# Attention with a message layer on one core: POOL makes three residuals before the attention and adds up a ninth tile in the first group of each chunk

## The reference

```
h    = relu(layernorm(x))
hs   = LN1(h);  ht = LN1(h_target)               # scale ln1_scale, bias ln1_bias
q    = (ht Wq + bq) / sqrt(32);  k = hs Wk + bk;  v = hs Wv + bv      # 8 heads of 32
p    = softmax over sources of (q k^T, -1e30 where there is no edge)
y    = LN2(ht + (p v) Wo + bo)
out  = x + y + gelu(y W1) W2                     # W1 256 x 1024, W2 1024 x 256
```

## Time and profile before

| | us |
|---|---|
| median of 3 runs | 499.89 |
| lowest, highest | 499.8, 501.54 |
| profiled execution | 502.69 |
| its span, first to last instruction | 500.8 |

### The profile page before, as it was taken

One profiled execution on the slowest core, in us unless ns is written; L12 is line 12 of the kernel. 1 busy time (PEld: TensorE's weight loads), 2 busy tenths in 40 slices (PEclk: granted clock), 3 DMA queues, 4 the chain that ended last, 5 costly groups with the idle time before them and its releaser, 6 DMA issues.

```text
span 500.8 us, 10602 instructions
## 1 busy us (share of the span) xinstructions
PE 477.0 (95%) x4364; PEld 245.4 (49%) x4364; DVE 416.5 (83%) x616; ACT 376.4 (75%) x455; POOL 309.9 (62%) x153
## 2 busy tenths in 40 slices
PE   3899979999999999999999999999999799999995
PEld 1466633333433343333433343333345688888884
DVE  5788579999999999999999999998997577565252
ACT  4786978998988998988998998999994370727150
POOL 2000008995998999999999998999999300000000
PEclk9899998999999999999999999999999899999998
DMA  8997689822633674222763300160000100202021
GB/s 254 250 192 115 125 247 403 297 43 44 211 58 55 68 172 80 43 45 48 82 171 66 64 3 3 36 178 2 1 1 3 45 21 23 84 2 84 0 85 45
DMA packets 53231, 46.94 MB, mean 94 GB/s; under 512 B 35454, under 2 KB 46108, under 8 KB 52668
## 3 DMA queue, kind: packets, MB, share of 16 engines
q1 hardware_dynamic: 50672, 37.30, 28.0%
q0 software_dynamic: 2480, 8.92, 10.7%
q10 hardware_dynamic: 28, 0.01, 0.0%
HBM read 31.93 MB, written 14.81 MB: 93 GB/s over the span
## 4 chain that ended last, share of the span: by engine, by line
PE 60%; DVE 16%; issue 13%; POOL 5%; ACT 4%; DMA 1%; DVEq 0%; POOLq 0%
PE acc L1316 13%; PE slot L1301 13%; DVE probs L971 10%; PE acc L1334 6%; PE slot L1416 3%; PE slot L1415 3%; PE slot L1414 3%; PE acc L1429 3%; PE acc L1431 3%; PE acc L1430 3%; PE slot L1214 3%; POOL added_up L527 3%; PE slot L1232 2%; PE slot L1367 2%; DVE stats L812 1%
## 5 line engine op out<-in xcount | busy, mean ns | idle before, releaser
L971 DVE SCALAR_TENSOR_TENSOR probs<-maskT,slot 128x1024 f32<-128x1024 uint16 x256 | 298.3, 1217 | 8.3 <-PE slot L1301 7.8
L713 ACT ACTIVATE probs<-probs 128x1024 f32<-128x1024 f32 x256 | 267.0, 1057 | 25.8 <-DVE probs L971 7.4
L527 POOL TENSOR_TENSOR added_up<-added_up,probs 128x1024 f32<-128x1024 f32 x96 | 226.7, 2401 | 1.2 <-ACT probs L713 1.0
L1316 PE MATMUL acc<-probs,V 128*32 128x512 f32 x1024 | 137.2, 608 | 1.0 <-ACT probs L713 1.0
L1334 PE MATMUL acc<-probs,ones 128*32 128x256 f32 x1024 | 77.1, 379 | 0.0
L1334 PEld LDWEIGHTS acc<-probs,ones 128*32 128x32 f32 x1024 | 33.3, 110 | 72.8 <-issue 71.2
L1301 PE MATMUL slot<-q_hi,k_hi 32*128 32x512 f32 x512 | 64.7, 496 | 3.8 <-DVE probs L971 3.5
L524 POOL TENSOR_TENSOR added_up<-probs 128x1024 f32<-128x1024 f32 x16 | 38.0, 2395 | 31.0 <-ACT probs L713 20.5
L1301 PEld LDWEIGHTS slot<-q_hi,k_hi 32*128 32x128 f32 x512 | 24.6, 182 | 62.1 <-DVE probs L971 55.3
L770 ACT ACTIVATE g_full<-slot 128x512 f32<-128x512 f32 x32 | 19.3, 602 | 46.9 <-issue 30.9
L1301 PE MATMUL slot<-q_lo,k_hi 32*128 32x512 f32 x512 | 52.0, 392 | 0.0
(11 more groups left out here) (130 smaller groups left out, 489.0 us busy)
## 6 DMA issues: line engine op xcount, KB each, us to landing
adj_raw<-in_adj POOLq DMA_DIRECT2D x16, 512.0 KB, 5.8
xs<-in_x SPq DMA_DIRECT2D x4, 512.0 KB, 7.0
htn<-in_L_gnn_h_target SPq DMA_DIRECT2D x4, 512.0 KB, 6.8
ht_saved<-htn SPq DMA_DIRECT2D x1, 2048.0 KB, 7.6
k_hi_saved<-k_hi SPq DMA_DIRECT2D x1, 2048.0 KB, 10.6
k_lo_saved<-k_lo SPq DMA_DIRECT2D x1, 2048.0 KB, 14.1
v_saved<-V SPq DMA_DIRECT2D x1, 2048.0 KB, 9.3
inverse<-inverse_saved SPq DMA_DIRECT2D x8, 256.0 KB
```

Of the source, the lines that this page charges most:

```text
L527: nc.gpsimd.tensor_tensor(added_up[:, pair], added_up[:, pair], at(i), ALU.add).then_inc(added, 1)
L713: nc.scalar.activation(p, p, ACT.Exp).then_inc(exped, 1)
L971: nc.vector.scalar_tensor_tensor(out=probs[:, u % RING], in0=m, scalar=-HALF_EDGE, in1=slot[u % SLOTS][:], op0=ALU.add, op1=ALU.min).then_ ...
L1316: mm = pe.matmul(acc[HD * j:HD * j + HD, 0, :], V[:, i, h * HD:(h + 1) * HD], probs[:, (PAIRS * k + j // 2) % RING, j % 2, :], start=(i == 0),
```

## The change

ADDED becomes a list for each group: FEWER (the eight tiles of before) for the second group of a chunk, MORE (these and tile 14) for the first. The counts that PE, DVE and POOL wait for follow from it (additions, added_through). PE then sums seven tiles in the first groups and eight in the second.

The residuals of chunks 0, 1 and 2 are made in front of POOL's attention loop, both steps of each, in place of one step behind each of the groups 0 to 5. The first step waits for the stored copy of its own chunk, for PE to have turned the chunk, and, for chunk 0, for DVE to have finished all target scales. SP stores htn by four DMAs, one for each chunk as it is normalised.

```diff
-    ADDED = [0, 1, 3, 5, 7, 9, 11, 13]
-    TAKEN = [i for i in range(ST) if i not in ADDED]
-    OPS = (len(ADDED) - 1) * PAIRS
+    FEWER = [0, 1, 3, 5, 7, 9, 11, 13]
+    MORE = FEWER + [14]
+    FIRST_TAKEN = 2
+    def added_in(G):
+        return FEWER if G % GROUPS else MORE
+    def is_added(k):
+        return k % ST in added_in(k // ST)
+    def additions(G):
+        return sum((len(added_in(n)) - 1) * PAIRS for n in range(G))
     def added_through(k, pair):
-        c, g, i = place(k)
-        return (c * GROUPS + g) * OPS + max(ADDED.index(i) - 1, 0) * PAIRS + pair + 1
+        G = k // ST
+        return additions(G) + max(added_in(G).index(k % ST) - 1, 0) * PAIRS + pair + 1
...
-        ht_kept = sem("ht_kept")
+        ht_kept = [sem(f"ht_kept{c}") for c in range(NCH)]
...
-            sp.wait_ge(normed_t, ST)
-            sp.dma_start(ht_saved, htn[:]).then_inc(ht_kept, 16)
+            for c in range(NCH):
+                sp.wait_ge(normed_t, TILES * (c + 1))
+                sp.dma_start(ht_saved[:, rows_of(c), :], htn[:, rows_of(c), :]).then_inc(ht_kept[c], 16)
...
                 if step == 0:
                     if c == 0:
                         pool.wait_ge(rest_made, 2)
-                        pool.wait_ge(ht_kept, 16)
+                        pool.wait_ge(norm_t, TARGET * NCH)
+                    pool.wait_ge(ht_kept[c], 16)
+                    pool.wait_ge(t_turned, c + 1)
...
+            for c in range(LAST):
+                make_residual(c, 0)
+                make_residual(c, 1)
             for c in range(NCH):
                 for g in range(GROUPS):
-                    for i in ADDED[1:]:
+                    for i in added_in(c * GROUPS + g)[1:]:
                         for pair in range(PAIRS):
                             add_up(c, g, i, pair)
...
                     if c and c < LAST:
                         divide(c - 1, g)
-                    if c < LAST:
-                        make_residual(c, g)
-                    elif g == 0:
+                    if c == LAST and g == 0:
                         divide(c - 1, 0)
                         divide(c - 1, 1)
...
-                    if place(previous)[2] in ADDED:
+                    if is_added(previous):
                         dve.wait_ge(added, added_through(previous, u % PAIRS))
...
             def close(G):
-                pe.wait_ge(added, OPS * (G + 1))
+                pe.wait_ge(added, additions(G + 1))
...
-                if k and (k - 1) % ST in TAKEN:
+                if k and not is_added(k - 1):
                     sum_weights(k - 1, 1)
-                if k % ST in TAKEN:
+                if not is_added(k):
                     sum_weights(k, 0)
```

More of the change, by code:

```diff
@@ L458, in _ @@
                 if c == LAST - 1:
-                    sp.wait_ge(ht_kept, 16)
+                    for n in range(NCH):
+                        sp.wait_ge(ht_kept[n], 16)
                     sp.wait_ge(q_kept, 32 * NCH)
@@ L520, in add_up @@
                 pool.wait_ge(exped, k * PAIRS + pair + 1)
-                if i == ADDED[1]:
+                if i == FEWER[1]:
                     if k >= ST:
                         pool.wait_ge(closed, c * GROUPS + g)
-                    nc.gpsimd.tensor_tensor(added_up[:, pair], at(ADDED[0]), at(i), ALU.add).then_inc(added, 1)
+                    nc.gpsimd.tensor_tensor(added_up[:, pair], at(FEWER[0]), at(i), ALU.add).then_inc(added, 1)
                 else:
@@ L555, in _ @@
                         n = c + 1 + g
[L556 to L559, removed]
+                        if i in (FEWER[4], FEWER[6]) and n < NCH and (c or g):
+                            load_adj(n, 2 - 2 * g + (i == FEWER[6]))
+                        elif i in (FEWER[4], FEWER[6]) and c == 0 and g == 0:
+                            load_adj(1, 2 + (i == FEWER[6]))
                     if c and c < LAST:
                         divide(c - 1, g)
-                    if c < LAST:
-                        make_residual(c, g)
-                    elif g == 0:
+                    if c == LAST and g == 0:
                         divide(c - 1, 0)
@@ L1320, in weigh @@
                     mm.then_inc(context_done, 1)
-                elif i in ADDED:
+                elif is_added(k):
                     mm.then_inc(used, 1)
@@ L1329, in sum_weights @@
                 ts = slice(half * CHUNK // 2, (half + 1) * CHUNK // 2)
-                first = i == TAKEN[0]
+                first = i == FIRST_TAKEN
                 if first and G and not half:
```

## The result

Beside the first runs of the change the kernel before took 500.54 us (median of 4), the changed one 512.50 us (median of 4, 510.61 to 514.27): ratio 1.0214, 95% interval 1.0179 to 1.0248. Run once more, in a later series, it was 1.0192 [1.0162, 1.0222], 510.72 against 501.06 us. One execution of the kernel before, in the series of the experiments, took 543.93 us at a mean granted clock of 0.845; it counts in no ratio and no fit. The profiled execution took 514.27 us with a span of 512.2, 11.4 more than before; its mean granted clock was 0.979 against 0.987.

A forecast was written before the change was run, and what follows sets the result against it. DVE and PE run neck and neck, POOL nearly full, its additions having 2.9 us to spare before group 2's close. Terms -0.4 + 2.0 + 2.0 + 4.7 + 1.4 = +9.7 on 499.9 give 509.6 us, range 506.5 to 512.3.

The forecast's parts named there:

- Residuals into the first stage: Six POOL residual instructions move before group 0, ending at 72.5, 3.2 us before POOL is needed: 0, bounds -0.2 to 0.2.
- Rival (c): First stage: residuals hold DVE's q_lo instructions, first masks up to 3.6 us later, 513.2 us; chance 0.08.
- Group 0: First group's close: POOL has 7.9 us of room against 4.7, so PE's saving shows: -0.4 us.
- the 3.1 left over: Group 0, before its close: POOL's 5.47 + 2.39 us to spare, less 4.7 of new additions, leaves 3.1 us.
- Groups 2 and 4: Their closes: POOL's additions for tile 14 end too late, PE closes late and DVE stands still: +2.0 us each.
- The last chunk: Groups 6 and 7: POOL starts group 7 later, and the attention's end follows POOL's chain through w2_lo: +4.7 us.
- the ring at tile 6: Group 7: DVE's mask of tile 6 needs tile 0's ring place, freed by POOL 4 us later than wanted.
- Rival (b): Group 7: a slack ring takes POOL's lateness off the path, only two closes and a spell paid, 504.9 us; chance 0.12.
- the two cases: End of attention: follows POOL by the shared-port rule, 4.7 us, or DVE if each engine were on its own, 4.0.
- The rule on the shared port: At L994: two-port VectorE instructions and GpSimd's block each other, so the stage's end follows POOL, 4.7 us rather than 4.0.
- The clock: PE idles 2.2 us before the closes of groups 2 and 4; one low-clock spell taken, +1.4 us, bounds 0 to 3.4.
- Rival (a): PE's wait on added in close: the additions hide, all four groups win 0.44, 498.1 us; chance 0.05.

The follow-up runs named there:

- the second profile: Profile of the changed kernel, unaltered, run again beside the kernel before: 510.72 against 501.06 us, ratio 1.0192.
- the experiment that has it alone: Changed kernel with the ninth added tile in group 6 only, residuals still in the first stage: 506.42 us, ratio 1.0098 to the kernel before.

## Why the prediction was right

It said 509.6 us where 512.5 and 510.7 were measured, and +9.7 us where the medians differ by 12.0 and 9.7. The range of 506.5 to 512.3 started from a median of 499.89; that times the measured ratio, 1.0214, is 510.6, inside it, while 512.5, beside a median of 500.54, is 0.2 above its end. That the second series meets +9.7 exactly is in part luck: without the clock the sum has +8.3, the two series have +7.7 and +6.8, and the clock's share was larger than its term. Step by step:

**Residuals into the first stage, 0.** Right: -0.1 +- 0.3. POOL was idle for 3.26 us before its first addition; 3.2 had been worked out. Rival (c) falls with it, and with the q_lo instructions, which kept their 1.41 us for two beside the residuals.

**Group 0, -0.4.** Right: -0.4 +- 0.3, and 2.77 to 2.32 us from tile to tile. POOL still waited 2.65 us for the close, of the 3.1 left over.

**Groups 2 and 4, +2.0 each.** Right: 40.11 against 38.20 in group 2, +1.9. Group 4 lost 2.8, the rest being the spell of low clock that began in the gap. In the second profile, without that spell, group 4 takes 273.34 - 233.26 = 40.08 us, +1.9. For groups 0, 2 and 4 together +3.4 +- 0.3 was measured against 3.6 in the sum.

**The last chunk, +4.7.** Right in place and nearly in size: 44.65 against 40.02 from group to group, +4.6, and +4.5 on POOL in the experiment that has it alone (+3.8 +- 0.4 at equal clock). The mechanism has two stations, as said: the ring at tile 6 (2.75 us of waiting before the first pair) and then L1011, held until w2_lo ended. Rival (b) falls. Their shares can be read too. DVE came to L1011 4.1 us later for the ring (78.06 against 73.95 us behind the first addition of group 6), and the hold by w2_lo added some 0.5 to make it POOL's 4.6; these are the 4.0 and the 4.7 that the prediction had for the two cases. Take the hold away in both kernels, and the change still costs 6.5 us. Take the ring's wait away (w1_lo inside group 7), and DVE is held by POOL's last additions instead: each station stands in for the other, because both follow POOL's list.

**The rule on the shared port.** I had weighed the row of 3.51 us against the page "Advanced Engine Details and Errata" of the Trainium skill, section "VectorE Performance Modes", by which two-port VectorE instructions and GpSimd's block each other. Moving w2_lo away shows that POOL was the cause in this kernel: 3.51 us became 0.17. The runs show that POOL's instruction held DVE's, which agrees with the page; that it was by the port they cannot show.

**The clock, +1.4.** The term was right for the spell that it named and too small for the series. One spell behind a close is in the first profile, at 276 us; groups 4 and 5 together take 317.11 - 237.26 = 79.85 us there and 311.62 - 233.26 = 78.36 in the second profile, which has none behind the closes: it cost 1.5 us. In the series the share of the clock is, by the fit, 12.0 - 7.7 = 4.3 us in the first and 2.7 in the second, hidden spells counted as if paid. It does not come from the two closes alone: the kernel with late closes in groups 2 and 4 and nothing in the last chunk has a mean clock of 0.989, that of the kernel before. Both kernels with the last chunk's stall and w2_lo in its old place beside the late closes run at 0.981 to 0.984. Which gap of theirs makes the difference I did not separate. In the first profile spells lie at 276 and at 400 to 408 us; but the one at 400 to 408, behind L1011, has its like at 392 to 396 in the kernel before, and those in the first stage and at the start of the attention stand in profiles of other kernels as well. So only the one at 276 is new there.

**The other side.** Rival (a) falls: POOL is later than PE in groups 2, 4 and 6, as PE's three waits for its additions show (2.13, 2.14 and 0.70 us).

## What to carry to other kernels

Ask of work taken off an engine on which side of that engine's deadline it stood. Six residual steps freed 14.3 us of POOL, but behind its additions, where it was waiting for PE anyway, and the added instructions stood in front of the wait, where 2.9 us were free and 4.7 were needed. So compare room and work group by group: only group 0 had both. Then look at what a small instruction on another engine waits for when it is absurdly long; here that pointed to 2 us in the old kernel that had nothing to do with the change. And a wait that comes from an overfull engine is not removed by moving work within its list, if the work still stands in front of what others wait for: the move of w1_lo only exchanged one wait for another.

## What the runs showed of the hardware that was not expected

DVE's L1011, on 128 x 4 values, was held over the boundary between two of POOL's back-to-back additions: 3.39 us, where one addition is 2.4 and the instruction alone takes 0.16 to 0.17. So POOL, in a row of such instructions, can hold a small instruction of DVE for longer than one instruction of its own. The masks, which read one operand from PSUM, ran at 1.17 us each beside the same additions.

Executions of one unchanged kernel lie up to 4.7 us apart with the share of low clock in them: 499.2 us at a mean clock of 0.996, 503.9 at 0.984. The same gap of PE, 1.74 us before the first keys, stands in all 13 profiles, and the eight matmuls behind it took 3.67 us in six of them (granted clock 1.00), 5.25 to 5.37 in five, and 6.55 and 6.68 in two. What decides between these the profiles do not show.
